# A graph network kernel: the second layer's bias products moved behind the edge loop, and the edge counts by destination summed by VectorE and transfers instead of TensorE

## What is computed

```python
A = zeros(N, N); A[src, dst] += edge_weight        # first layer: weighted adjacency
dinv = where(A.sum(1) > 0, A.sum(1) ** -0.5, 0)
h = x
for l in range(2):
    h = (dinv[:, None] * A * dinv[None, :]) @ h
    h = leaky_relu((h @ W_gcn[l] + b_gcn[l]) @ W_mlp[l] + b_mlp[l])
x = layernorm(x + h)
# second layer: C counts the edges, self loops included; deg1 = its column sums (edges by destination)
dis = deg1 ** -0.5
g = lambda x, W, b: dis * (C.T @ ((x @ W) * dis)) + b
x = layernorm(x + g(relu(g(x, W1, b1)), W2, b2))
```

## Time and profile before

| | |
|---|---|
| median of 3 runs | 331.31 us (331.01 to 331.38) |
| profiled execution, its time | 331.32 us |
| its span in the trace | 329.5 us |
| TensorE busy | 310.8 us, 94% of the span |
| VectorE / ScalarE / GpSimd busy | 185.4 / 121.9 / 49.9 us |
| granted TensorE clock, mean | 0.999 |

### The profile page before, as it was taken

The page is one execution under the profiler, slowest core; times in us unless marked ns, Lnnn a source line. Parts: engine busy times, 40 slices in busy tenths (PEclk is TensorE's granted clock), DMA queues, the critical chain, the costliest instruction groups (busy, mean ns, idle before and its releaser), DMA issues.

```text
span 329.5 us, 4860 instructions
## 1 busy us (share of the span) xinstructions
PE 310.8 (94%) x1945; PEld 255.9 (78%) x1945; DVE 185.4 (56%) x329; ACT 121.9 (37%) x253; POOL 49.9 (15%) x54
## 2 busy tenths in 40 slices
PE   2968999998999999999999999999999999999993
PEld 1756886887788888888888888888888888888882
DVE  6998999723544511255542376767913444225664
ACT  3638798645433510133422031316502554220000
POOL 2100000002004980200000012121760000001111
PEclk9999999999999999999999999999999999999999
DMA  6283300200020000000802000008000000000121
GB/s 194 85 285 79 89 0 2 66 2 2 3 64 1 2 0 0 2 0 0 251 6 64 0 2 0 0 2 288 5 0 2 0 0 0 2 4 32 66 92 67
DMA packets 11070, 14.49 MB, mean 44 GB/s; under 512 B 4130, under 2 KB 4514, under 8 KB 11044
## 3 DMA queue, kind: packets, MB, share of 16 engines
q1 hardware_dynamic: 11044, 14.11, 13.7%
HBM read 12.00 MB, written 2.11 MB: 43 GB/s over the span
## 4 chain that ended last, share of the span: by engine, by line
PE 88%; DVE 7%; issue 2%; ACT 1%; DMA 1%; POOLq 0%; POOL 0%; SPq 0%; ACTq 0%
PE psum L677 76%; PE psum L735 6%; PE psum L663 3%; DVE hot L1017 2%; PE psum L782 1%; DVE sel L1009 1%; DVE hot L1012 1%; PE psum L719 1%; DVE wm_low L1102 1%; DVE wgt_low L1089 1%; DMA src_i<-in_src 1%; PE psum L741 1%; ACT hot L482 1%; PE psum L880 1%; PE psum L775 0%
## 5 line engine op out<-in xcount | busy, mean ns | idle before, releaser
L468 POOL TENSOR_TENSOR small<-small 128x1 f32<-128x1 f32 x16 | 11.9, 743 | 160.0 <-DVE small L1277 160.0
L735 PEld LDWEIGHTS psum<-hot,sel 128*128 128x128 bf16 x512 | 28.4, 101 | 6.7 <-issue 6.1
L735 PE MATMUL psum<-hot,sel 128*128 128x96 bf16 x512 | 32.1, 214 | 1.5 <-DVE hot L1017 1.3
L677 PE MATMUL psum<-at_high,x_high 128*128 128x512 f32 x64 | 25.8, 403 | 0.6 <-DVE x_low L1213 0.6
L1089 DVE SCALAR_TENSOR_TENSOR y_low<-psum,small,y_high 128x512 fp32r<-128x512 f32 x16 | 11.9, 750 | 24.2 <-ACT y_high L482 24.2
L1089 DVE SCALAR_TENSOR_TENSOR g_low<-psum,g_high 128x512 fp32r<-128x512 f32 x16 | 10.2, 683 | 26.7 <-ACT g_high L482 26.7
L677 PE MATMUL psum<-at_low,x_high 128*128 128x512 f32 x64 | 25.1, 392 | 0.0
L677 PE MATMUL psum<-cnt,x_high 128*128 128x512 f32 x64 | 25.0, 390 | 0.0
L677 PE MATMUL psum<-at_high,x_low 128*128 128x512 f32 x64 | 24.9, 390 | 0.0
L677 PE MATMUL psum<-cnt,x_low 128*128 128x512 f32 x64 | 24.9, 389 | 0.0
L677 PE MATMUL psum<-y_high,at_high 128*128 128x512 f32 x64 | 24.9, 389 | 0.0
(11 more groups left out here) (181 smaller groups left out, 743.2 us busy)
## 6 DMA issues: line engine op xcount, KB each, us to landing
wg_raw<-in_L_gnn_W_gcn SPq DMA_DIRECT2D x2, 1024.0 KB, 5.5
x_raw<-in_x SPq DMA_DIRECT2D x8, 256.0 KB, 2.6
xs<-in_x SPq DMA_DIRECT2D x1, 2048.0 KB, 16.4
w_raw<-in_L_gnn_W SPq DMA_DIRECT2D x2, 1024.0 KB, 7.2
out<-xs SPq DMA_DIRECT2D x8, 256.0 KB, 2.1
wm_raw<-in_L_gnn_W_mlp SPq DMA_DIRECT2D x1, 1024.0 KB, 8.4
wm_next<-in_L_gnn_W_mlp SPq DMA_DIRECT2D x1, 1024.0 KB, 8.9
col_scale<-scales SPq DMA_DIRECT2D x2, 512.0 KB, 4.5
```

Source lines behind the costliest of these rows:

```text
L468: pool.tensor_tensor(r[:, 1:2], r[:, 0:1], power[:, 0:1], ALU.pow).then_inc(rstd_ready, 1)
L677: ins = pe.matmul(dest, s, m, start=first and n == 0, stop=end and n == len(pairs) - 1, skip_group_check=True)
L735: ins = pe.matmul(sums[1 if k == 0 else 0], stationary, moving, start=False, stop=False, skip_group_check=True)
```

## The change

Three things.

- In the table of fillers `bias1` and `biasb1` are gone from the loop (they stood at chunks 66 and 73); `wc1`'s pieces move one place forward each, the piece at 99 shrinks from six multiplies to three, a piece of three is new at 118, and six instead of twelve are left behind the last chunk. `bias1` is now done behind the third `turn_adjacency`, ahead of the first pass of `g1_a`, and `biasb1` between the first and second pass, with a row buffer of its own (`next_rows`). Since they also stand elsewhere in the list of banks, the blocks `at` 0 to 2 have other banks than before.
- The multiplies by the column of ones are gone. Behind the first `lower` of `g1_b`, VectorE waits for `cnt_sums`, turns it in 32x32 blocks, half by half, and sums within each block (32 part sums for each of 128 partitions), turns those, and SyncE writes them to memory in four transfers of 32x32 words and reads them back as [32 x 4 x 32]; VectorE adds the four, GpSimd makes `dis` on 32 partitions of 32 columns, and two more transfers bring it to [128 x 8] by way of `scales`.
- In SyncE's queue, the second write of `scales` no longer stands behind the load of `xs`; all of the above stands ahead of it.

```diff
@@ -244,10 +255,10 @@
                    27: [("wc0", 0, 0, KD)], 31: [("wc0", 1, 0, KD), ("prep", 4, 0, KD)], 34: [("wc0", 2, 0, 2)],
                    40: [("wc0", 2, 2, KD), ("wc0", 3, 0, 2)], 47: [("wc0", 3, 2, KD), ("bias0", 0, 0, KD)],
                    53: [("biasb0", 0, 0, KD), ("wgt1", 0, 0, KD), ("wgt1", 1, 0, KD)],
-                   60: [("wgt1", 2, 0, KD), ("wgt1", 3, 0, KD)], 66: [("bias1", 0, 0, KD)],
-                   73: [("biasb1", 0, 0, KD), ("wc1", 0, 0, 2)], 79: [("wc1", 0, 2, KD)], 86: [("wc1", 1, 0, 2)],
-                   92: [("wc1", 1, 2, KD)], 99: [("wc1", 2, 0, 2)], 105: [("wc1", 2, 2, 3)], 112: [("wc1", 2, 3, KD)],
-                   CH - 1: [("wc1", 3, 0, KD)]}
+                   60: [("wgt1", 2, 0, KD), ("wgt1", 3, 0, KD)], 66: [("wc1", 0, 0, 2)],
+                   73: [("wc1", 0, 2, KD)], 79: [("wc1", 1, 0, 2)], 86: [("wc1", 1, 2, KD)], 92: [("wc1", 2, 0, 2)],
+                   99: [("wc1", 2, 2, 3)], 105: [("wc1", 2, 3, KD)], 112: [("wc1", 3, 0, 1)], 118: [("wc1", 3, 1, 2)],
+                   CH - 1: [("wc1", 3, 2, KD)]}
         stops = sorted(set(closing) | set(fillers))
         filling = [(name, i) for c in sorted(fillers) for name, i, k0, k1 in fillers[c] if k1 == KD]
...
@@ -263,6 +274,8 @@
         for name, i in filling:
             in_ring(name, i, FILL)
         for j in range(NB):
+            if j in (2, 3):
+                in_ring("bias1" if j == 2 else "biasb1", 0, FILL)
             in_ring("at", j, FILL)
         n_fill[0] = 0
         for name, count in (("at_b", NB), ("g1_b", KD)):
...
@@ -375,28 +390,44 @@
                     sp.wait_ge(x_in, 16 * n)
                 sp.dma_start(x_raw[:, j, :], x[j * P:(j + 1) * P, :]).then_inc(x_in, 16)
             sp.wait_ge(done["biasb0"], 1)
-            sp.dma_start(bias_rows[2:3, :], bm[1:2, :]).then_inc(bm_in, 16)
-            sp.wait_ge(done["biasb1"], 1)
             sp.wait_ge(scaled, G * len(SHARED))
             for j in range(X_LATE):
                 sp.dma_start(x_raw[:, j, :], x[j * P:(j + 1) * P, :]).then_inc(x_in, 16)
-            def spread(n, columns):
+            sp.wait_ge(region_done, 1 + closing.index(99))
+            sp.dma_start(next_rows[2:3, :], bm[1:2, :]).then_inc(bm_in, 16)
+            def scales_to_memory(n, columns):
                 with nc.allow_non_contiguous_dma(reason="nodes' scales"):
                     sp.dma_start(scales[n].rearrange("(b p) -> p b", p=P), columns).then_inc(scales_out, 16)
+            def rows_from_memory(n):
                 sp.wait_ge(scales_out, 16 * (n + 1))
                 sp.dma_start(col_scale[:], scales[n:n + 1, :].broadcast_to([P, N])).then_inc(scales_in, 16)
             sp.wait_ge(loop_done, 1)
             sp.wait_ge(adj_ready, 1)
             sp.wait_ge(dinv_ready, 1)
-            spread(0, dinv)
+            scales_to_memory(0, dinv)
+            rows_from_memory(0)
+            sp.wait_ge(part_turned, 1)
+            for g in range(P // Q):
+                sp.dma_start(counted[g].rearrange("(c j) -> c j", j=Q), turned_sums[g * Q:(g + 1) * Q, :])\
+                    .then_inc(counted_out, 16)
+            sp.wait_ge(counted_out, 16 * (P // Q))
+            sp.dma_start(part_rows, counted.rearrange("g (c j) -> c g j", j=Q)).then_inc(counted_in, 16)
+            sp.wait_ge(pow_ready, 2)
+            sp.dma_start(scales[1].rearrange("(c j) -> c j", j=Q), dis_rows).then_inc(scales_out, 16)
+            sp.wait_ge(scales_out, 32)
+            with nc.allow_non_contiguous_dma(reason="nodes' scales"):
+                sp.dma_start(dis, scales[1].rearrange("(b p) -> p b", p=P)).then_inc(dis_in, 16)
             sp.wait_ge(done["h1"], 2 * KD)
             sp.dma_start(xs[:], x.rearrange(by_k, p=P)).then_inc(x_again_in, 16)
             sp.wait_ge(taken["h1"], 2 * KD)
-            sp.wait_ge(pow_ready, 2)
-            spread(1, dis)
+            rows_from_memory(1)
             sp.wait_ge(done["h2"], NB)
             sp.dma_start(w1_raw[:], w1.rearrange(by_k, p=P)).then_inc(w1_in, 16)
             sp.dma_start(w2_raw[:], w2.rearrange(by_k, p=P)).then_inc(w2_in, 16)
...
@@ -459,8 +490,9 @@
                 add_loops(cnt_all, cnt_all[:])
             with pool.Else():
                 add_loops(cnt, cnt[:].bitcast(F32))
-            pool.wait_ge(taken["deg1"], 1)
-            to_power(deg1, dis, NB)
+            pool.wait_ge(deg1_ready, 1)
+            pool.tensor_tensor(dis_rows, loops_rows, power[0:Q, 0:1].broadcast_to([Q, Q]), ALU.pow)\
+                .then_inc(pow_ready, 1)
             def to_rstd(b, count):
                 pool.wait_ge(var_ready, count)
...
@@ -581,6 +612,9 @@
                 upper_x(j)
                 if j + 1 < NB:
                     upper_at("at", 0, j + 1)
+                if j in (1, 2):
+                    upper_fill("bias1" if j == 1 else "biasb1", 0)
             for j in range(NB):
                 upper_at("at_b", 1, j)
             for f in range(KD):
...
@@ -757,9 +793,10 @@
                 elif name.startswith("wc"):
                     l = int(name[-1])
                     s = slice(i * P, (i + 1) * P)
-                    if i == 0 and k0 == 0:
-                        pe.wait_ge(wm_low_ready, KD * (l + 1))
-                        pe.wait_ge(low_made[f"wgt{l}"], KD)
+                    if i == 0:
+                        if k0 == 0:
+                            pe.wait_ge(wm_low_ready, KD * (l + 1))
+                        pe.wait_ge(low_made[f"wgt{l}"], k1)
                     ins = split_product(b, [(wgt_high[:, k, s], wgt_low[:, k, s]) for k in range(k0, k1)],
                                         [(wm_high[:, k, :], wm_low[:, k, :]) for k in range(k0, k1)],
                                         first=(k0 == 0), end=(k1 == KD))
...
@@ -852,6 +889,7 @@
             for j in range(3):
                 turn_adjacency("at", 0, j)
+            filler("bias1", 0, 0, KD)
             pe.wait_ge(evacuated, copies(NR - 1))
             for j in range(NB):
                 pe.wait_ge(low_made["at"], j + 1)
...
@@ -864,6 +902,8 @@
                         ins.then_inc(done["g1_a"], 1)
                 if j + 3 < NB:
                     turn_adjacency("at", 0, j + 3)
+                if j == 0:
+                    filler("biasb1", 0, 0, KD)
                 if j >= 4:
                     for k in range(2 * (j - 4), 2 * (j - 3)):
                         turn_adjacency("at_b", 1, k)
...
@@ -873,12 +913,6 @@
                               [at_parts(1, j) for j in range(NB)],
                               ready=(lambda j: pe.wait_ge(low_made["at_b"], j + 1)) if f == 0 else None)\
                     .then_inc(done["g1_b"], 1)
-            pe.wait_ge(sums_added, NB - 1)
-            b = claim("deg1")
-            for n in range(NB):
-                ins = pe.matmul(b[:, n:n + 1], cnt_sums[:, n * P:(n + 1) * P], ones_col, start=True, stop=True)
-            ins.then_inc(done["deg1"], 1)
             def feature_rows(name, wh, wl, gh, gl, ready):
                 for n in range(2 * KD):
...
@@ -1226,10 +1260,25 @@
                 lower_at("at_b", 1, j)
             for f in range(KD):
                 lower("g1_a", f, g1_low[:, f, 0:BANK], bank("g1_a", f), g1_high[:, f, 0:BANK])
-            for f in range(KD):
+            def lower_g1_b(f):
                 lower("g1_b", f, g1_low[:, f, BANK:], bank("g1_b", f), g1_high[:, f, BANK:])
-            dve.wait_ge(done["deg1"], 1)
-            dve.tensor_copy(deg1, bank("deg1")[:, 0:NB]).then_inc(taken["deg1"], 1)
+            lower_g1_b(0)
+            dve.wait_ge(sums_added, NB - 1)
+            for h in range(2):
+                if h:
+                    dve.wait_ge(sums_ready, h)
+                dve.transpose(turned_cnt, cnt_sums[:, h * BANK:(h + 1) * BANK]).then_inc(sums_turned, 1)
+                dve.wait_ge(sums_turned, h + 1)
+                dve.tensor_reduce(part_sums[:, h * (BANK // Q):(h + 1) * (BANK // Q)],
+                                  turned_cnt.rearrange("p (c i) -> p c i", i=Q), AX.X, ALU.add).then_inc(sums_ready, 1)
+            dve.wait_ge(sums_ready, 2)
+            dve.transpose(turned_sums, part_sums).then_inc(part_turned, 1)
+            for f in range(1, KD):
+                lower_g1_b(f)
+            dve.wait_ge(counted_in, 16)
+            dve.tensor_reduce(loops_rows, part_rows.rearrange("p g j -> p j g"), AX.X, ALU.add).then_inc(deg1_ready, 1)
             rows = [0, 0]
```

More of the change, by code:

```diff
@@ L29 @@
 R = 2
+Q = 32
 def gnn_resnorm(nc, x, src, dst, weight, wg, bg, wm, bm, w1, b1, w2, b2, out):
@@ L141, in gnn_resnorm @@
         late_ends = at("late_ends", B2, [P, 2, NB, NR - 1 - LATE_END, WINDOW], F32)
+        next_rows = at("next_rows", B2, [3, D], F32)
         again(B2)
@@ L212, in gnn_resnorm @@
         cnt_sums = at("cnt_sums", SM, [P, N], F32)
+        turned_cnt = tmp[:, 2, :]
+        part_rows = tmp[0:Q, 2, 0:P].rearrange("p (g j) -> p g j", j=Q)
         used = [0]
@@ L221, in gnn_resnorm @@
```

(23 more changed lines are left out.)

1 line of the change is left out of this document (added).

## The result

The median went from 331.29 us (6 runs, 331.01 to 331.38) to 329.68 us (6 runs, 329.57 to 329.87): ratio 0.9955, 95% interval 0.9945 to 0.9965, or 1.6 us less. Forecast were 329.4 and a gain of 1.9. The profiled execution took 329.61 us with a span of 327.8.

What follows compares the result with a forecast made beforehand. TensorE, busy 310.8 of 329.5 us, was taken to bound the kernel. The bias part (-0.25) and the counts (-1.71) gave -1.96, taken as -1.9 after an idle-time cross-check: 331.3 - 1.9 = 329.4 us, range 328.7 to 330.6.

Steps and rivals of the forecast that it cites:

- The counts: Ahead of h1, the eight multiplies by ones leave TensorE: 1.71 us saved, the replacement work hidden.
- The transfers as a rival: Short-piece transfers of the part sums are slow and h1's first row waits: 337.9 us, chance 8%.
- The tolerance of 5 us: In h1 and y1, TensorE tolerates the first row of h1 coming 5 us late without losing time.
- The estimate from the same section for the turning: VectorE's turning of the counts at 2.5 us each; part sums 3.6 us later, still within what TensorE tolerates.
- rival (a): Read-back of part sums at 11.2 us a hop, 13.5 late, 8.5 beyond the tolerance: 337.9 us, chance 8%.
- Behind the loop: From loop's end to second pass: 1.7 us idle, first pass 1.3 earlier, biasb1 costs 1.05 to 1.07; -0.25 left.
- The loop, the mis-sized term: Edge loop from chunk 66 on: fillers removed or shrunk end it 1.97 us earlier, at 75.78.
- 0.13 charged at chunk 122: Three new multiplies behind chunk 118, 0.78 us, replace the 0.65 wait at chunk 122: 0.13 lost.
- Rival (b): Edge loop shortens by less, ScalarE's copies making the clears wait: 330.7 us at most, 330.2 middle, chance 12%.
- the bias part: Moved fillers and bias products, in and behind the edge loop, together worth -0.25 us.

Runs made afterwards that it cites:

- counts_alone: The kernel before with only the new sums of the counts and SyncE's new order, fillers and bias products unchanged: 329.32 us, ratio 0.9940.
- hops3: The changed kernel with the write and read-back of the part sums done three times in a row: 329.89 us, 0.9957 of the kernel before.
- hops5: The changed kernel with the write and read-back of the part sums done five times in a row: 338.06 us, 1.0200 of the kernel before.
- scale_first: The changed kernel with ScalarE scaling its columns at chunk 73 ahead of copying out the wc1 tile: 329.50 us, 0.9941 of the kernel before.
- gap_banks: The changed kernel with bias1 ahead of the third turned block and both bias products in bank 4: 328.13 us, 0.9910 of the kernel before.

## Why the prediction was right, and where it was off

The time lies in the range and the direction holds. By its steps:

- **The counts** (-1.71): right, shown by counts_alone (-1.9 in the median). The new operations cost 0.71 and 0.69 each where 0.69 was taken from the nearest row, and the last reduce 0.36. The part sums were there at 126.0 (125.7 forecast), the read-back at 130.4 (130.8).
- **The transfers as a rival**: they were not slow. A hop of 128-byte runs landed in 1.4 to 1.6 us, not the 8 at which the sign would have turned. The Trainium skill's warning in "VectorE: DVE Perf Modes", section "The three transpose paths", of a plain strided copy 19 times slower, is given there for a large innermost stride at the destination; the innermost runs here are 128 contiguous bytes, and no such cost shows in them. The estimate from the same section for the turning, 2.5 us, was 3.5 times too high: 0.71 for 128x512 words of four bytes, and the measurement decides.
- **The tolerance of 5 us** in `h1`: the number held, the place did not. hops3 (3.2 late, 0.3 of it because this execution started later) loses nothing, hops5 (12.5 late) pays, so the tolerance lies between the two. The prediction took it from row 8 and tile 4 (5.1 in the changed kernel: wanted at 168.03, there at 162.92); the waits of hops5 stand in tile 0, which needs row 4 and tolerates 5.85 (157.15 against 151.30). What was left out is the clock: beyond the tolerance hops5 paid 2.2 us more than its lateness. The price of rival (a), 8.5 us for 13.5 of lateness, was by this too low.
- **Behind the loop**: right to 0.1. The wait ahead of the third block, ended by `at_low`, was 1.58 (1.7 forecast), the stretch from the loop's end to the first pass 6.41 (82.2 - 75.78 = 6.42 forecast), and the second bias product took 1.12 with its restart where 1.06 was reckoned.
- **The loop, the mis-sized term**: -1.97 was forecast, -1.42 measured, 0.55 short. The savings of TensorE's work hold: 0.38, 1.06 and 0.69 behind chunks 66, 73 and 99, for 0.38, 1.07 and 0.70. What failed is the step "Behind chunk 73, `biasb1` and six multiplies took 2.55, now six, 1.48: 1.07 saved", which credits the whole saving to the loop: TensorE arrived at chunk 80 before ScalarE's scaling of the batch, and the sum has no term for that. I had not asked what ScalarE now does at chunk 73. The two gaps that follow from it, 0.23 and 0.25 longer, make 0.48, and scale_first closes them. Another 0.2 is at chunk 105, where the gap behind three multiplies was 0.47 and is 0.69 now, put down to issue; at this place TensorE's program also reads the offsets of the chunks from 112 on (`load_offsets`), in both kernels, but why the gap grew was not tried. The other way, 0.13 charged at chunk 122 was not lost: the new piece takes 0.79, and from the last chunk ahead of the clear to the clear it is 0.22 instead of 1.02. Rival (b), a loop shortened by less since ScalarE's work bounds it, thus happened in part, by scaling where I had named copies.

So the bias part was forecast at -0.25 and was +0.3 to +0.35: its sign was wrong, and the total lies in the range because the counts, the far larger part, came as forecast. Its stated effect, TensorE work moved out of a busy loop, took place; what it frees is given back since one of the moved products stands behind the wait it could have filled, and the other in a stretch with no idle time. gap_banks shows the first: filling the wait, with the other bank for the third block, is worth 1.5 us.

## What to carry to other kernels

Work moved into a gap fills it only if it stands ahead of the instruction that waits and needs nothing (operand or buffer) that the wait is for; the list that assigns buffers counts as such a need, near the place and some blocks later. Before crediting an engine with time saved in a loop, read what the other engines do at the same points, for a copy that now falls ahead of something urgent. A small sum that costs the busiest engine 1.7 us can go over idle engines and several transfers of 128-byte runs, if the wait stands where the work behind it has some microseconds to spare; beyond these, hops5 paid for the waits and for slower multiplies behind them.

## What was not expected of the hardware

- TensorE's clock fell in hops5 during its second wait in `y1`: it had waited 0.84 us, done three multiplies at the usual distance of 0.23 to 0.34 (156.84 to 157.42) and then waited 2.24. The granted clock is 1.00 up to 157, 0.81 in the stretch 157 to 160 and 0.50 (the 1.2 GHz level) from 160 to 169; it is 0.98 from 169 to 172, after TensorE had worked without a wait from 163.25 on. At the low level multiplies are 0.43 apart instead of 0.23. In the changed kernel the same load of `xs` runs beside `y1` and the clock stays at 1.00, so the load alone is not the cause. A wait of 1.58 us by itself, in the changed kernel, shows no such fall (granted 1.00 in every stretch from 74 to 89). A stall's price then is more than its length: 2.8 us of slower multiplies here.
- 1024 pieces of four bytes read from memory into `dis` landed after 2.3 us, while `dinv`, the same number of pieces written to memory, held the next issue from 78.95 to 87.61 (8.7 us). In the kernel before the two writes of this kind took 9.6 and 12.9 us to the next issue (80.58 to 90.14, 160.64 to 173.53), the second beside the load of `xs`. For these transfers the write is the slow direction.
- The load of `src_i` at the start is awaited until 3.00 to 3.55 us in the ten profiled executions of this study, up to 0.55 us that have nothing to do with the edits.
